# A two-layer gated block: the two bias products of each hidden pair on 64 array rows each, issued together

## The reference

```
x = x + tanh(g_xattn[0]) * L0_xattn(layernorm(x), ctx)
x = x + tanh(g_ffn[0])   * L0_ffn(layernorm(x))
x = x + tanh(g_xattn[1]) * L1_xattn(layernorm(x), ctx)
x = x + tanh(g_ffn[1])   * L1_ffn(layernorm(x))        # 8 experts, top 2, capacity 512
```

```
h   = x @ w1 + b1                # 256 -> 1024
h   = round to multiples of 2^-8
h   = piecewise linear gelu(h)   # 33 knots on [-4, 4], quantised
out = round(h @ w2 + b2)         # 1024 -> 256
```

## Time and profile before

| | |
|---|---|
| median of 3 runs | 510.99 us (510.92 to 511.07) |
| span of the profiled execution | 509.3 us |
| difference of the two | 1.7 us |
| PE busy | 479.0 us (94%) |
| DVE busy | 383.8 us (75%) |
| ACT busy | 258.0 us (51%) |
| bias products L1687 | 32, 389 ns each in the records, 13.0 us |
| TensorE clock, mean granted | 0.987 |

### The profile page before, as it was taken

How to read it: one execution, slowest core, us unless ns; L and a number is a source line. 1 busy time by engine, 2 the same in 40 slices (tenths; PEclk the granted TensorE clock), 3 DMA queues, 4 the chain that set the end, 5 groups by cost and what they waited for, 6 DMA issues and landing times.

```text
span 509.3 us, 8629 instructions
## 1 busy us (share of the span) xinstructions
PE 479.0 (94%) x3258; PEld 407.4 (80%) x3258; DVE 383.8 (75%) x771; ACT 258.0 (51%) x396; POOL 147.5 (29%) x123
## 2 busy tenths in 40 slices
PE   6999999999999999999999759999999999999991
PEld 4777789898887777777777528988999998999991
DVE  4799999899998867979778896557667575748441
ACT  2667788776865654555546314344434443444120
POOL 4364100010001202212013127115072827354253
PEclk9999999999999999999999979999999999999997
DMA  6523000000000001210311543035364737372041
GB/s 209 157 83 73 24 2 1 0 1 1 1 2 0 24 19 42 84 54 31 125 42 42 167 134 98 18 72 143 105 137 145 154 105 164 94 168 47 1 42 20
DMA packets 37166, 36.06 MB, mean 71 GB/s; under 512 B 6458, under 2 KB 35974, under 8 KB 36998
## 3 DMA queue, kind: packets, MB, share of 16 engines
q1 hardware_dynamic: 30665, 27.65, 17.6%
q0 software_dynamic: 6144, 7.66, 9.1%
q10 hardware_dynamic: 317, 0.21, 0.1%
HBM read 27.70 MB, written 8.39 MB: 71 GB/s over the span
## 4 chain that ended last, share of the span: by engine, by line
PE 65%; DVE 23%; issue 6%; ACT 3%; DMA 2%; POOL 1%; DVEq 0%; ACTq 0%; POOLq 0%
PE PS L1477 14%; PE PS L1478 14%; PE PS L1479 14%; PE PS L1893 5%; PE PS L1837 4%; PE PS L1750 3%; DVE tmp L1139 3%; DVE tmp L1128 3%; DVE hT_lo L1147 3%; PE PS L1497 3%; PE PS L1902 3%; DVE tmp L1116 1%; DVE xn L995 1%; DVE nmaxC L1170 1%; DVE tmp L1119 1%
## 5 line engine op out<-in xcount | busy, mean ns | idle before, releaser
L1477 PE MATMUL PS<-w_hi,hT_hi 128*128 128x256 f32 x384 | 110.3, 287 | 0.1
L1479 PE MATMUL PS<-w_hi,hT_lo 128*128 128x256 f32 x384 | 108.6, 283 | 0.0
L1478 PE MATMUL PS<-w_lo,hT_hi 128*128 128x256 f32 x384 | 108.6, 283 | 0.0
L939 ACT ACTIVATE tmp<-PS,biasT 128x512 f32<-128x512 f32 (+1 forms) x80 | 43.8, 600 | 111.0 <-PE PS L1479 111.0
L664 POOL DMA_INDIRECT out<-tmp,dst_idx x32 | 55.8, 1744 | 99.5 <-DVE tmp L1433 92.8
L1477 PE MATMUL PS<-xT_hi,w_hi 128*128 128x512 f32 (+1 forms) x224 | 81.1, 362 | 0.4 <-DVE xT_lo L1003 0.4
L1478 PE MATMUL PS<-xT_lo,w_hi 128*128 128x512 f32 (+1 forms) x224 | 80.7, 360 | 0.0
L1479 PE MATMUL PS<-xT_hi,w_lo 128*128 128x512 f32 (+1 forms) x224 | 80.5, 359 | 0.0
L1477 PEld LDWEIGHTS PS<-w_hi,hT_hi 128*128 128x128 f32 x384 | 73.4, 191 | 3.3 <-issue 2.3
L1478 PEld LDWEIGHTS PS<-w_lo,hT_hi 128*128 128x128 f32 x384 | 73.5, 191 | 0.8
L1479 PEld LDWEIGHTS PS<-w_hi,hT_lo 128*128 128x128 f32 x384 | 73.5, 191 | 0.0
(11 more groups left out here) (261 smaller groups left out, 865.8 us busy)
## 6 DMA issues: line engine op xcount, KB each, us to landing
w_raw<-in_L_ffn_w SPq DMA_DIRECT2D x72, 256.0 KB, 3.3
residual<-in_x SPq DMA_DIRECT2D x4, 512.0 KB, 5.5
out<-residual SPq DMA_DIRECT2D x3, 512.0 KB, 4.5
normed_rows<-xn SPq DMA_DIRECT2D x3, 512.0 KB, 2.9
kv<-in_L_ffn_b SPq DMA_DIRECT2D x1, 1024.0 KB, 6.6
tmp<-in_L_xattn_Wq SPq DMA_DIRECT2D x2, 256.0 KB, 5.6
out<-residual SPq DMA_DIRECT2D x2, 256.0 KB, 5.1
normed_rows<-xn SPq DMA_DIRECT2D x2, 256.0 KB, 4.0
```

The costliest lines, as they stand in the source:

```text
L939: act.activation(gD[:, G % 2, f, 0:P * n], H[:, G % 2, f, 0:P * n], ACT.Gelu, bias=biasT[:, col:col + 1]).then_inc(e_gelu, 1)
L1477: pe.matmul(o, lh, rh, start=start, stop=False, skip_group_check=skip)
L1478: pe.matmul(o, lh, rl, start=False, stop=False, skip_group_check=skip)
L1479: return pe.matmul(o, ll, rh, start=False, stop=stop, skip_group_check=skip)
```

## The change

Each of the two bias products of a pair uses 64 rows of the array: f = 0 the rows 0 to 63, f = 1 the rows 64 to 127. For this the bias rows stand twice in `bias_hl` (high parts also in rows 64 to 71, low parts in rows 96 to 103), and `pick_row` has ones there too. Both products are issued one behind the other before the twelve others of the pair; before, the second stood in the middle. Two more small loads, three more DVE operations and two small POOL operations make the operands.

```diff
-        N_CTX, N_V0, N_LATER = 2, 4, 9
+        N_CTX, N_V0, N_LATER = 2, 4, 11
...
-            for row in (0, 32):
+            for row in (0, 32, 64, 96):
                 later(b1_rows[row:row + 8, :], rows(b1_0))
...
-            pool.tensor_tensor(pick_row, bcast(ident[:, 0:8].unsqueeze(2), [P, 8, P]),
-                               bcast(ident[:, 32:40].unsqueeze(2), [P, 8, P]), ALU.add).then_inc(pick_ready, 1)
+            pool.tensor_tensor(small[:, 0:8], ident[:, 0:8], ident[:, 32:40], ALU.add)
+            link(pool.tensor_tensor(small[:, 8:16], ident[:, 64:72], ident[:, 96:104], ALU.add))
+            pool.tensor_tensor(pick_row, bcast(small[:, 0:8].unsqueeze(2), [P, 8, P]),
+                               bcast(small[:, 8:16].unsqueeze(2), [P, 8, P]), ALU.add).then_inc(pick_ready, 1)
...
-                dve.tensor_copy(bias_hl[0:8, :], b1_rows[0:8, :])
-                link(dve.tensor_copy(bias_hi[32:40, :], b1_rows[32:40, :]))
-                dve.tensor_tensor(bias_hl[32:40, :], b1_rows[32:40, :], bias_hi[32:40, :].bitcast(F32),
-                                  ALU.subtract).then_inc(bias_split, 1)
+                for row in (0, 64):
+                    dve.tensor_copy(bias_hl[row:row + 8, :], b1_rows[row:row + 8, :])
+                    ins = dve.tensor_copy(bias_hi[row + 32:row + 40, :], b1_rows[row + 32:row + 40, :])
+                link(ins)
+                for row in (32, 96):
+                    dve.tensor_tensor(bias_hl[row:row + 8, :], b1_rows[row:row + 8, :],
+                                      bias_hi[row:row + 8, :].bitcast(F32), ALU.subtract).then_inc(bias_split, 1)
...
-                    pe.wait_ge(bias_split, 1)
+                    pe.wait_ge(bias_split, 2)
                     pe.wait_ge(pick_ready, 1)
+                for f in range(2 if g < NB_PAIRS else 0):
+                    half = slice(64 * f, 64 * f + 64)
+                    pe.matmul(H[:, g % 2, f, :].rearrange("p (a b) -> p a b", a=4),
+                              bias_hl[half, :], bcast(pick_row[half, 2 * (g % PAIRS) + f, :].unsqueeze(1), [64, 4, P]),
+                              start=True, stop=False)
                 for f in range(2):
-                    if g < NB_PAIRS:
-                        pe.matmul(H[:, g % 2, f, :].rearrange("p (a b) -> p a b", a=4),
-                                  bias_hl, bcast(pick_row[:, 2 * (g % PAIRS) + f, :].unsqueeze(1), [P, 4, P]),
-                                  start=True, stop=False)
```

## The result

The changed kernel takes 512.46 us (median of 5 runs, 512.32 to 513.89) against 510.99 in the same session: a ratio of 1.0032 with the interval 1.0021 to 1.0043, or +1.6 us (+1.1 to +2.2). The forecast was 511.7 us within 510.9 to 512.9. The range holds the time, but "slower by over 0.2%" came true, and that had 0.33, not the 0.64 of "within 0.2%". The profiled execution has a span of 510.4 us against 509.3.

The account below looks back on a forecast made before the run. PE and DVE were taken as nearly full, PE's cost counting only where others wait: +0.17 us a pair, less gaps, gives +0.73, rounded to 0.75, setup nothing; 510.99 + 0.75 = 511.74, so 511.7 us, range 510.9 to 512.9.

Parts of the forecast that it names:

- +0.17 us a pair: PE at each pair's head: two side-by-side 64-row bias products with their border cost 0.63 us against 0.46 before.
- entering: From the last full-row product to a pair's first bias product: +0.09 us over the ordinary distance.
- first bias product to first full product: Head of a pair: 0.34 load and stream, 0.01 second product's start, 0.09 leaving; 0.44 us.
- the next full product: Step after a pair's first full product, whose load isn't ahead: +0.10 us.
- From a pair to the stage: 15 pairs cost 2.5 us of PE time; gaps take part, copy 0 is 0.46 late, copy 2 0.75.
- one behind the other: Rival at the pair's head: bias products don't run side by side, +0.39 us a pair, 514.5 us; chance 0.10.
- the first gap: PE's 0.73 us free before the transposes after hidden(5), taken off the 0.85 us of pairs 1 to 5.
- The rest of the kernel gives nothing back: After chunk 2, DVE and ACT set the pace to the second attention; the fixed order gives none of the delay back.
- Setup "put at nothing": Kernel start: added loads, DVE and POOL work, 0.6, 0.7 and some 0.4 us without cover, taken as covered.
- The carried 1.7 us: Whole kernel: median of the runs lies 1.7 us above the profiled span, carried over to the forecast.
- Swallowed: Rival in the stage: border costs less (+0.06 a pair) or waits have more room; 511.2 to 511.4 us; chance 0.18.
- No border: Rival at the pair's head: 64 rows bring no border, -0.22 us a pair, 510.5 us; chance 0.08.

Follow-up runs that it names:

- E5: Kernel before with a third full-row bias product at the head of each pair, overwritten by the next: 512.62 us, ratio 1.0029.
- E4: Kernel before with 64-row bias products at the head of the pair, both on the same rows 0 to 63: 515.71 us, ratio 1.0092.
- E6: Kernel before with PE's gate weights moved behind project(3), and ACT's copy of them behind its copy of chunk 0: 510.20 us, ratio 0.9980.
- E2: Kernel before with the change's loop of 64-row products but the old setup: 511.99 us, ratio 1.0021.
- E1: Kernel before with all of the change's new setup but the old full-row products: 511.44 us, ratio 1.0003.
- E9: Kernel before with one added tiny DVE write of zero to a column of small: 511.51 us, one run.

## Why the prediction came out as it did

**The cost of a pair: right in its steps, 0.04 us too small in sum.** Of "+0.17 us a pair" the steps at the border hold. Averages over the pairs, predicted and measured: entering +0.09 and +0.09; first bias product to first full product 0.44 and 0.42; the next full product +0.10 and +0.11. Together 0.16 us. The second bias product starts 0.003 us behind the first; I had put 0.01. Missing is what comes after. I let the distances return to the ordinary ones behind the second full product. They do not: the next ten take 2.33 us in sum instead of 2.28. That makes +0.21 us a pair (3.30 us from the last project product to the last of hidden, 3.09 before). This is the term that was mis-sized.

For the rule that the prediction weighed, the Trainium skill (TensorEngine Tiling (Array Packing), Key Properties) says that a change of the tiling mode drains TensorE; the rows of the changed kernel agree, with loads that never start ahead over the border. The same section's "Tiles operate independently" agrees too, with the 0.003 us. What decides is the size of the one against the other. Running side by side saves 0.23 us a pair, and the border costs 0.44.

**From a pair to the stage: right.** With 0.21 in place of 0.17 the prediction's own way gives 0.74 us for the copy of chunk 0 and 1.1 for that of chunk 2; it stands so beside the rival "one behind the other", as the point from which 0.2% is passed. Measured from pair 0 on, DVE's additions are 0.64, 0.64 and 1.04 us late. The pattern is the predicted one: the first gap swallows most of five pairs, chunk 0 is late by what is left, chunk 1 adds nothing, chunk 2 adds 0.40. E5 shows it with an undisputed cost, E4 with a large one, E6 for the narrow place. Of the 3.1 us of PE time that the 15 pairs behind pair 0 cost (15 x 0.21), 1.04 reach the end of the stage.

**The rest of the kernel gives nothing back: right.** E2 has +0.04 us there.

**Setup "put at nothing": right at its place, wrong far from it.** The loads, POOL's work and DVE's copies delay nothing at the start beyond the scatter of the start itself: E1 begins pair 0 0.59 us earlier than the kernel before, E2, which has none of the setup, also 0.59 earlier. But DVE's three added instructions bring the pause of 0.35 us in the routing. No row of the kernel before showed this, and the prediction had no term for it.

**The carried 1.7 us: misread, without effect.** I set the median of before against the span of another execution, the profiled one. Wherever an execution's time and its own span are both on record, in all kernels, the time is 1.7 to 2.2 us longer, 2.1 in the median, and so it is for the changed kernel. By that the profiled execution of before took some 511.4 us (509.3 + 2.1, an estimate), 0.4 more than the median. The forecast adds 0.75 to a median and doesn't hang on this. The spans differ by 1.1 and not by 1.4 because the profiled execution of the changed kernel began pair 0 0.32 us earlier.

Summed up: 1.04 in the stage and 0.34 behind it are 1.4 us, inside the timed +1.6 (1.1 to 2.2). The forecast had 0.75. Of the missing 0.65, 0.3 are the mis-sized pair and 0.35 the unforeseen pause. The range held the time, but as far as the pause goes that was luck: nothing in the range was meant for it. The pair's part is backed by the timed runs of E2 (+1.1 us, 0.6 to 1.6); the pause is not, as said.

**The rivals.** "Swallowed" is out: 0.21 is far from its 0.06, and DVE is late at all three chunks. "One behind the other" is out by the 0.003 us, and E4 shows what it would have been. "No border" is out by the loads.

## What to carry to other kernels

Two products on half the rows run at the same time, but each trip into a 64-row tiling and back costs about 0.44 us here, in distances and late loads, so two products of 512 columns (0.23 us saved) lose 0.21; by these numbers it would take four products per trip, two and two side by side, to come out level (2 x 0.23 against 0.44, an estimate that no run tried). Before costing such an edit, find the copies that wait for PE and the gaps before them: 3.1 us of PE time became 1.04 here, and 0.9 us came back from moving work that nobody waits for from in front of one copy to behind it. A difference of a few tenths can sit far from the edit, so measure by stage and not by the end alone.

## What was not expected of the hardware

- Distances of 512-column products stay at 0.233 us for ten products behind the border instead of 0.228. Why is open; in E4, with the same border, the ten take 2.29 us in sum, between the two.
- A pause of 0.35 us on DVE at a place that depends on how many instructions stand ahead. Counting DVE's records in the trace, semaphore events with them, the instruction behind the pause is the 704th in all four kernels that have it in the routing; in the kernel before, the 704th is one of the operations of 0.6 to 0.7 us that follow (L1348), where no pause is seen. In E9 the instruction behind the pause is the 448th, 256 earlier.
- A possible reason, which no run tests: the loading of instructions. The traces record packets of 8192 bytes on one of the two instruction queues, 14 or 15 of them after the first 5 us of a trace. In all thirteen traces one of them starts within 1 us of DVE's 448th, 576th and 704th instruction each, and 0.7 to 1.0 us after the one behind a pause.
